# A graph-network layer on one core: the sum R taken ahead of the scaling T, and one copy of b2 moved behind hi

## The reference

```python
h   = maximum(layernorm(x), 0)
agg = segment_sum(edge_attr_128, src, num_segments=50000)
t   = silu(concatenate([h, agg], -1) @ W1 + b1)      # 256 -> 256
t   = t @ W2 + b2                                    # 256 -> 128
out = x + (layernorm(t) * ln_gamma + ln_beta + h)
```

## Time and profile before

| | |
|---|---|
| median of 3 runs | 780.91 us (779.41 to 783.76) |
| the profiled execution | 779.33 us, span 777.7 us, granted clock 0.987 |
| TensorE matmul busy | 719.1 us (92%) |
| VectorE busy | 706.2 us (91%) |
| ScalarE busy | 629.1 us (81%) |
| GpSimd busy | 488.9 us (63%) |
| DMA | 65.89 MB, 85 GB/s on average |

### The profile page before, as it was taken

One profiled execution on the slowest core, in us unless ns is written; L12 is line 12 of the kernel. 1 busy time (PEld: TensorE's weight loads), 2 busy tenths in 40 slices (PEclk: granted clock), 3 DMA queues, 4 the chain that ended last, 5 costly groups with the idle time before them and its releaser, 6 DMA issues.

```text
span 777.7 us, 15386 instructions
## 1 busy us (share of the span) xinstructions
PE 719.1 (92%) x4554; PEld 594.4 (76%) x4554; DVE 706.2 (91%) x2275; ACT 629.1 (81%) x2034; POOL 488.9 (63%) x414
## 2 busy tenths in 40 slices
PE   7999998789999999999999999999999999999994
PEld 3555546668888888888888888888888888888883
DVE  8999997889898989898989898989898989898988
ACT  7999975568878788788887887888878887878793
POOL 3000017567877777777787777777877777777730
PEclk9999999799999999999999999999999999999997
DMA  5000000123332323232323232323332323222112
GB/s 201 1 2 1 2 4 23 46 73 104 102 104 103 103 104 102 103 105 101 103 102 104 101 102 99 106 101 103 104 102 101 103 102 106 103 91 80 50 65 78
DMA packets 28265, 65.89 MB, mean 85 GB/s; under 512 B 8473, under 2 KB 10028, under 8 KB 28180
## 3 DMA queue, kind: packets, MB, share of 16 engines
q1 hardware_dynamic: 15604, 51.90, 18.0%
q0 software_dynamic: 12576, 12.99, 6.6%
HBM read 52.05 MB, written 25.60 MB: 100 GB/s over the span
## 4 chain that ended last, share of the span: by engine, by line
DVE 33%; issue 33%; PE 13%; another core or an unknown queue 13%; ACT 6%; DVEq 0%
DVE stat L823 9%; DVE T L1034 7%; PE y L657 4%; ACT hi L548 4%; DVE lo L1022 2%; PE za L652 2%; PE pre L652 2%; PE za L645 2%; PE pre L645 2%; DVE R L1029 1%; DVE var L863 1%; DVE R L1004 1%; DVE guess L867 1%; ACT hi L546 1%
## 5 line engine op out<-in xcount | busy, mean ns | idle before, releaser
L435 POOL DMA_INDIRECT G<-in_edge_attr_dram,slot_edge x388 | 478.6, 1234 | 152.6 <-issue 110.3
L740 PEld LDWEIGHTS y<-w2c,S 128*128 128x128 f32 (+1 forms) x1556 | 189.9, 193 | 10.8 <-issue 2.8
L740 PE MATMUL y<-w2c,S 128*128 128x128 f32 (+1 forms) x1556 | 191.1, 276 | 2.1 <-ACT S L555 2.1
L1022 DVE TENSOR_TENSOR lo<-za,hi 128x1024 fp32r<-128x1024 f32 (+1 forms) x98 | 119.0, 1214 | 60.0 <-ACT hi L548 53.4
L538 ACT ACTIVATE H<-X,shift,rstd 128x128 f32<-128x128 f32 x392 | 163.8, 513 | 2.9 <-DVE shift L882 2.4
L715 PE MATMUL pre<-hi,w1h 128*128 128x512 f32 (+1 forms) x392 | 163.4, 417 | 2.3 <-issue 1.2
L716 PE MATMUL pre<-hi,w1l 128*128 128x512 f32 (+1 forms) x392 | 154.8, 395 | 0.4 <-issue 0.4
L555 ACT ACTIVATE S<-pre,b1c 128x512 f32<-128x512 f32 (+1 forms) x196 | 128.5, 731 | 12.0 <-remote 8.7
L720 PE MATMUL pre<-lo,w1h 128*128 128x512 f32 (+1 forms) x392 | 123.2, 395 | 0.2
L546 ACT CAST hi<-za 128x512 fp32r<-128x512 f32 (+1 forms) x98 | 59.5, 607 | 71.0 <-remote 67.7
L701 PE MATMUL za<-HOT,G 128*128 128x128 f32 (+1 forms) x784 | 104.8, 277 | 1.8 <-issue 1.1
(11 more groups left out here) (154 smaller groups left out, 1005.5 us busy)
## 6 DMA issues: line engine op xcount, KB each, us to landing
X<-in_x_dram SPq DMA_DIRECT2D x48, 512.0 KB
out_dram<-R SPq DMA_DIRECT2D x48, 512.0 KB
G<-in_edge_attr_dram,slot_edge POOLq DMA_INDIRECT x388
X<-in_x_dram SPq DMA_DIRECT2D x1, 424.0 KB
out_dram<-R SPq DMA_DIRECT2D x2, 192.0 KB
w1f<-in_L_gnn_W_dram SPq DMA_DIRECT2D x1, 256.0 KB
w2f<-in_L_gnn_W_dram SPq DMA_DIRECT2D x1, 128.0 KB
srci<-in_src_dram SPq DMA_DIRECT2D x1, 85.8 KB
```

The lines of the kernel that those rows point to most:

```text
L435: nc.gpsimd.indirect_dma_start(G[b.j][:, t, :], None, source, bass.IndirectOffsetOnAxis(ap=slot_edge[:, bass.ds(b.number(TILES, t), 1)], a ...
L740: done = nc.tensor.matmul(places[t][0:r], S[c][:, m, t * r:(t + 1) * r], w2c[:, m, :], start=False, stop=True, skip_group_check=True)
L1022: nc.vector.tensor_tensor(out=lo[c][:, :, w], in0=za[:, :, w], in1=hi[c][:, :, w].bitcast(F32), op=ALU.subtract).then_inc(lo_done, 1)
```

## The change

VectorE in step b first does `result(b-3)`, both halves, and then `scale(b-2)`, both halves. Before, it did `scale(b-2)` and then `result(b-2)`. So the sum over T is taken one step after T was made, and T of a half is overwritten just after it was read (new waits on `out_done` in `scale`, on VectorE's own earlier instruction). R lives a step longer: four buffers in place of three, and SyncE stores block b-3 in step b. On ScalarE the copy of b2 for a first half, `bias(b, 0)`, stands behind `split_high(b+1, 0)` and no longer ahead of it; that of a second half stays. Three of GpSimd's eight pacing points per block move with VectorE's new order: the first gather of a step waits for `result(b-3)`, the second for the first half of T, the third for the second half of T. TensorE's list is unchanged. The last step does `result` of two blocks.

```diff
+R_RING = 4
-        R = [sb(f"R{j}", [P, TILES, D], F32) for j in range(RING)]
+        R = [sb(f"R{j}", [P, TILES, D], F32) for j in range(R_RING)]
...
             def step(b):
                 if b.plus(X_AHEAD).exists(NB):
                     load(b.plus(X_AHEAD))
-                if not b.is_number(0) and not b.is_number(1):
-                    store(b.plus(-2))
+                if b.plus(-3).exists(NB):
+                    store(b.plus(-3))
...
             def pace(b, c, k):
 
                 if c == 0 and k == 0:
-                    at_least(pool, lo_done, b.half(1, 1, 1))
+                    at_least(pool, out_done, b.plus(-3).half(1, 1, 1))
                 elif c == 0 and k == 1:
                     at_least(pool, t_done, b.plus(-2).half(0, 1, 1))
                 elif c == 0 and k == 2:
-                    at_least(pool, out_done, b.plus(-2).half(0, 1, 1))
+                    at_least(pool, t_done, b.plus(-2).half(1, 1, 1))
...
                     if ahead.exists(NB):
                         split_high(ahead, 1 - c)
+                    if c and b.half(0) >= RAMP:
+                        bias(b, 0)
...
                     if b.half(c) >= RAMP:
                         silu(b, c)
-                        if not b.is_number(NB - 1) or not c:
+                        if not b.is_number(NB - 1) and c:
                             bias(b, c)
...
             def x_plus_beta(b):
                 dve.wait_ge(x_loaded[b.xj], b.x_lap(16, 16))
-                at_least(dve, stored[b.j], b.lap(16))
+                at_least(dve, stored[b.rj], b.r_lap(16))
...
             def scale(b, c):
 
                 dve.wait_ge(powers_done, b.number(1, 1 + POWERS_LAG))
+                at_least(dve, out_done, b.half(c, 1, -1))
...
                 else:
+                    if b.plus(-3).exists(NB):
+                        for c in range(2):
+                            result(b.plus(-3), c)
                     for c in range(2):
                         scale(b.plus(-2), c)
-                    for c in range(2):
-                        result(b.plus(-2), c)
+                    if b.is_number(NB - 1):
+                        for c in range(2):
+                            result(b.plus(-2), c)
                 if b.plus(1).exists(NB):
                     split_low(b.plus(1), 0)
```

More of the change, by code:

```diff
@@ L80, in xj, with rj, r_lap @@
         return self.ring(X_RING)
+    @property
+    def rj(self):
+        return self.ring(R_RING)
+    def r_lap(self, factor, more=0):
+        return self.group(R_RING, factor, more)
     def x_lap(self, factor, more=0):
@@ L252, in gnn_layer @@
         x_loaded = [sem(f"x_loaded{j}") for j in range(X_RING)]
-        stored = [sem(f"stored{j}") for j in range(RING)]
+        stored = [sem(f"stored{j}") for j in range(R_RING)]
         gathered = [[sem(f"gathered{j}{c}") for c in range(2)] for j in range(RING)]
@@ L329, in store @@
                 sp.dma_start(out[bass.ds(b.number(BLOCK), rows * TILES), :]
-                             .rearrange("(p t) d -> p t d", t=TILES), R[b.j][0:rows]).then_inc(stored[b.j], 16)
+                             .rearrange("(p t) d -> p t d", t=TILES), R[b.rj][0:rows]).then_inc(stored[b.rj], 16)
             for n in range(X_AHEAD):
@@ L337, in step @@
                     load(b.plus(X_AHEAD))
-                if not b.is_number(0) and not b.is_number(1):
-                    store(b.plus(-2))
+                if b.plus(-3).exists(NB):
+                    store(b.plus(-3))
             run_blocks(step)
+            store(Block(NB - 3))
             store(Block(NB - 2))
@@ L347, in _ @@
                 for rows in LAST_PARTS:
-                    sp.dma_start(to[rows, s, :], R[last.j][rows, s, :]).then_inc(stored[last.j], 16)
-            for j in range(RING):
-                sp.wait_ge(stored[j], 16 * (len(range(j, NB, RING)) + (j == last.j) * (2 * len(LAST_PARTS) - 1)))
+                    sp.dma_start(to[rows, s, :], R[last.rj][rows, s, :]).then_inc(stored[last.rj], 16)
+            for j in range(R_RING):
+                sp.wait_ge(stored[j], 16 * (len(range(j, NB, R_RING)) + (j == last.rj) * (2 * len(LAST_PARTS) - 1)))
         @block.gpsimd
@@ L1002, in x_plus_beta @@
                 dve.wait_ge(x_loaded[b.xj], b.x_lap(16, 16))
-                at_least(dve, stored[b.j], b.lap(16))
-                nc.vector.tensor_tensor(out=R[b.j][:], in0=X[b.xj][:],
+                at_least(dve, stored[b.rj], b.r_lap(16))
+                nc.vector.tensor_tensor(out=R[b.rj][:], in0=X[b.xj][:],
                                         in1=betas[:].unsqueeze(1).to_broadcast([P, TILES, D]),
@@ L1028, in residual @@
                 dve.wait_ge(h0_done, b.half(1, 1, 1))
-                nc.vector.tensor_tensor(out=R[b.j][:], in0=H0[b.j][:], in1=R[b.j][:], op=ALU.add).then_inc(r_done, 1)
+                nc.vector.tensor_tensor(out=R[b.rj][:], in0=H0[b.j][:], in1=R[b.rj][:], op=ALU.add).then_inc(r_done, 1)
             def scale_tile(b, c, t):
@@ L1050, in result @@
                 s = slice(c * HALF, (c + 1) * HALF)
-                nc.vector.tensor_tensor(out=R[b.j][:, s, :], in0=T[c][:], in1=R[b.j][:, s, :],
+                nc.vector.tensor_tensor(out=R[b.rj][:, s, :], in0=T[c][:], in1=R[b.rj][:, s, :],
                                         op=ALU.add).then_inc(out_done, 1)
@@ L1139, in last_result @@
                 nc.vector.scalar_tensor_tensor(
-                    out=R[last.j][:, n, :], in0=last_place(c, t), scalar=rstd[last.ring(POWERS_LAG)][:, TILES + n:TILES + n + 1],
-                    in1=R[last.j][:, n, :], op0=ALU.mult, op1=ALU.add).then_inc(last_out, 1)
+                    out=R[last.rj][:, n, :], in0=last_place(c, t), scalar=rstd[last.ring(POWERS_LAG)][:, TILES + n:TILES + n + 1],
+                    in1=R[last.rj][:, n, :], op0=ALU.mult, op1=ALU.add).then_inc(last_out, 1)
             def beside_first(place):
+                if place == 0:
+                    dve.wait_ge(out_done, last.half(1, 1, -3))
                 if place < HALF:
```

## The result

Beside the kernel before, the changed kernel took 869.8 us (median of 4 runs, 863.0 to 882.0) against 780.2 (778.8 to 783.8): ratio 1.111, 95% interval 1.103 to 1.120. The prediction said 754, in a range of 738 to 815. The profiled execution took 871.97 us, its span 870.4, at a granted clock of 0.942 in place of 0.987.

What follows compares the result with a forecast made beforehand. It took a chain of waits between TensorE, ScalarE and VectorE as the bound, 12.89 us a block. Saving 0.62 us 43 times, 26.7 us, from 779.33 gave 752.6, 754 on the median's scale; range 738 to 815.

Steps and rivals of the forecast that it cites:

- its open point: Between the transposes' row end and ScalarE's `hi` of a second half: 2.42 us, agreeing with a late acknowledgement, cause unknown.
- The test named for a wrong forecast: At ScalarE: the forecast is wrong if `hi` still starts 2.4 us or more after the transposes' row has ended.
- GpSimd gains about 1.07 us per block ... that is worth 0 by itself: GpSimd's gather at R no longer takes 2.07 us but 1.00; no wait of TensorE names it, so 0.
- the forecast: R in place of T beside the transposes lets `hi` start early: 26.7 us saved, 754 us; chance 0.41.
- the second rival: TensorE's signal is late until VectorE has left PSUM: 834 us, or up to 794; chance 0.30.
- The first rival: TensorE's signal to `hi` is late for its own reasons: no change, 779 to 781 us; chance 0.29.
- VectorE's period: VectorE's time per block with `hi` at once and `lo` following T at 494.0: from 12.89 to 11.85 us.
- Swap and copy at 0 each: VectorE's R ahead of T, and ScalarE's copy of b2 behind `hi`: each said to cost 0.
- TensorE's floor of 12.27 us: TensorE's busy time per block, below which its period can't fall; limits the saving to 0.62 us per block.

Runs made afterwards that it cites:

- e15: Changed kernel with GpSimd's first gather released by the first of the two sums R, not the second: 723.3 us, 1.002 times the kernel before.
- e17: Changed kernel with GpSimd's first gather released by the first of the two sums R, not the second, again: 723.4 us, 1.002 times the kernel before.
- e12: Changed kernel without the 376 paced gathers, edge sums of blocks 2 to 48 left out: 725.7 us, 0.942 times the kernel before.
- e5: Changed kernel without the paced gathers of blocks 2 to 48, edge sums left out: 723.5 us, 1.002 times the kernel before.
- e1: Kernel before with only ScalarE's copy of b2 for a first half moved behind `hi`: 722.2 us.
- e2: Changed kernel with only the copy of b2 put back ahead of `hi`: 750.0 us, 1.039 times the kernel before.
- e3: Changed kernel with GpSimd's first gather released by `lo` of the second half, as before: 782.9 us, 1.015 times the kernel before.
- e13: Changed kernel with an idle iota on GpSimd in front of three of a block's eight gathers: 780.8 us, 1.011 times the kernel before.
- e6: Changed kernel unedited, timed again beside the kernel before: 849.0 us.

## Why the prediction was wrong

*What bounds the kernel.* The chain (`lo`, transposes, signal, `hi`, `lo`) was the right one, and the loss sits on exactly its open point, the signal after the transposes. The test named for a wrong forecast, `hi` 2.4 us or more after the row's end, is met with 6.26.

*The step that failed* is "GpSimd gains about 1.07 us per block ... that is worth 0 by itself". The gain came: gathers fell from 1234 to 1071 ns. But the new release of the first gather, from which it comes in part, costs some 66 us in a slow session: putting it back alone took the changed kernel from 849.0 to 782.9, its gathers then taking 1153 ns. Whether their shorter time or their place does it isn't shown, since e15 and e17 fell in quick sessions. I priced GpSimd by its own queue (is it full, does anyone wait for G) and not by what its gathers do beside TensorE.

*The cause of the late signal* was put on VectorE, in the forecast (R in place of T beside the transposes) and in the second rival. Both are refuted: T may stand beside the transposes with `hi` 0.03 us behind them (e12), and the signal stays away while VectorE idles (494.56 to 497.17). Nor does SBUF work beside the transposes keep their signal prompt, as the forecast took from the earlier trace rows. In the changed kernel the half with R beside it is prompt (rows' end 500.98, signal 500.99), but GpSimd stands still there; the hold is now in the other half, and beside its transposes of 490.34 VectorE makes a sum on SBUF tiles too (R from x and beta, 489.74 to 490.95). The first rival, TensorE's own reasons, pointed the right way with the earlier trace rows, but priced as no change. In the earlier trace rows, the gather that runs at R takes 2.07 us and `hi` starts inside it, and so do all 40 held `hi` of that trace, inside gathers of 1.9 to 2.1 us; that was in the rows, and I read it as GpSimd's loss.

*The second rival's price*, 834, is the nearest to the result, but by accident: its mechanism isn't what happened, and the result is 36 us above it and 55 above the range. (A slip beside this: `lo` at 494.0 in place of 494.99 makes VectorE's period 11.90, not 11.85. It changes nothing, as the sum went by TensorE's 12.27.)

*Swap and copy at 0 each.* As a pair right to 1.5 us (e15, e5). Apart, the copy is 0 (e1), but the swap alone costs 28 us (e2). I had worked out the copy's place only from the side of its own lateness.

*TensorE's floor of 12.27 us* was mis-sized: without gathers a block takes 11.82 (e12), VectorE's busy time. The 12.27 held at least 0.45 us that a block doesn't need; in e15, with the gathers and without late signals, a block takes 11.83 too (500 us for 338 gathers, eight a block).

*The clock* was in no term. TensorE's busy time rose by 36 us, and behind a long wait its transposes take 1.12 us in place of 0.60 at a granted clock of 0.50.

The Trainium skill (Perfetto Trace Analysis, Tensor Engine Instruction) says that a matmul's semaphore goes out after PSUM has acknowledged. That agrees with signals later than the rows; it names nothing that would hold one for 6 us, and what the runs add is that in the one slow session where the gathers were taken out it was gone.

*Shown*: `hi` waits for signals that TensorE raises late (the semaphores' times), the holds need the gathers (e12), and the release of one gather (e3) or pauses (e13) take most of the change's loss away. *Argued only*: that a hold feeds itself, because a VectorE that stands can't start the sum beside which the next gather would stall. That a hold lasts until GpSimd's gathers pause or stall fits the kernel before and one trace of the changed kernel, and not e6; what ends a hold is open. Gathers back to back don't suffice either: in the timeline above TensorE's signals at 487.34 and 488.74 were raised at once, with gathers running since 485.63, and in quick sessions none is late beside the same gathers.

*Open*: what makes a session slow. In all three slow sessions, the first measurement included, the unedited changed kernel was among those run, and in none of the four quick ones; if the two things had nothing to do with each other, that would happen once in 35 times. A rival that nobody tested is the recording: events are missing by the hundred in just the traces that have late signals, and every time here comes from an execution with a recorded span and clock, so whether the holds are there without it isn't known. The kernel before without gathers never fell in a slow session, nor did the copy alone, so how much of its 49 us hangs on the gathers, and what makes the 12 us that e3 keeps, isn't shown.

## What to carry to other kernels

An engine off the critical path can still slow the one on it, so when a row says "remote" or a signal comes late, look at what every other engine does beside it, and vary that alone. The times at which semaphores were raised, where a trace keeps them, tell a late signal from a late waiter. Removing stalls from a stream of indirect DMAs is no free gain; test the releases apart from the reordering they came with. And time the unedited kernel in each session: here 722 and 771 us of one kernel would have swallowed or faked any change under 6%.

## What the runs showed of the hardware

- TensorE's completion signals can come 6 us late while GpSimd issues gathers back to back (129 of 298 by over 1 us), and those of VectorE and ScalarE in the same trace don't (0.02 us at most); without gathers, in a slow session too, TensorE's come within 0.015 us of the row's end (e12).
- In the long holds TensorE stops as well. In the timeline above it had executed 4 + 8 + 12 + 7 = 31 matmuls since the transposes began, and did one more after the first held signal had gone out (495.70). The waits above have 40 such stops inside or ahead of layer2 (L752 for "issue"), 20.0 us; in the kernel before no wait of layer2 is among those of the same stretch.
- One kernel has two times 6 to 7% apart (721.9 and 769.8) in two sessions on chip 4; with its gathers taken out the changed kernel doesn't (723.4 and 725.7).
